# Neighbour layer of a four-layer convolution kernel: one banded matrix per source row, and one shifting transfer per direction

## What is computed

```python
avg = mean(x, axis=channels)
df = abs(conv3x3(avg, laplacian, zero_padding))
k = 1 + round((df - min(df)) / (max(df) - min(df) + 1e-8) * 7)   # per position, min and max per image
patches = unfold3x3_reflect(x)                 # B, C, 9, P
sim = sum_c(x/|x| * patches/|patches|)         # B, 9, P: cosine of each position with its 9 neighbours
w = exp(sim) for the k most similar neighbours, else 0
w = w / sum(w)
enhanced = sum_k(patches * w) + group_norm16(x, gn_weight, gn_bias)
layer1 = enhanced + w2 @ relu(w1 @ enhanced + b1) + b2
```

## Time and profile before

| | |
|---|---|
| median of 3 runs | 5874.34 us (5872.79 to 5879.55) |
| profiled execution, its own time | 5873.65 us |
| its span, first to last instruction | 5871.9 us |
| mean granted TensorE clock | 0.907 of full speed |
| layer 1 in the span | about 2575 to 3600 us |
| TensorE matmuls busy in the whole span | 82% |
| VectorE busy in the whole span | 70% |

### The profile page before, as it was taken

The page is one execution under the profiler, slowest core; times in us unless marked ns, Lnnn a source line. Parts: engine busy times, 40 slices in busy tenths (PEclk is TensorE's granted clock), DMA queues, the critical chain, the costliest instruction groups (busy, mean ns, idle before and its releaser), DMA issues. The chain is left out here.

```text
span 5871.9 us, 127208 instructions
## 1 busy us (share of the span) xinstructions
PE 4826.6 (82%) x46150; PEld 3795.6 (65%) x46150; DVE 4095.5 (70%) x7785; ACT 3137.9 (53%) x5832; POOL 2837.5 (48%) x2148
## 2 busy tenths in 40 slices
PE   2887878787878787842876875999997999999996
PEld 1655555555656565622544543777777999999996
DVE  5767777776767777767987956999984555555554
ACT  1666666565656566641433424666653544456664
POOL 1535454453535454432543524888882333333364
PEclk9888989898988898965988987999998999999998
DMA  4000000000000000022433421011103000000357
GB/s 146 16 31 16 31 16 31 16 25 22 21 26 17 26 20 16 16 70 91 133 124 102 134 70 53 35 46 41 43 32 134 0 0 0 0 0 0 29 49 151
DMA packets 359128, 268.74 MB, mean 46 GB/s; under 512 B 289440, under 2 KB 290720, under 8 KB 352544
## 3 DMA queue, kind: packets, MB, share of 16 engines
q1 hardware_dynamic: 355264, 258.30, 15.4%
q10 hardware_dynamic: 3424, 4.59, 0.2%
HBM read 156.27 MB, written 67.11 MB: 38 GB/s over the span
## 5 line engine op out<-in xcount | busy, mean ns | idle before, releaser
L527 POOL TENSOR_TENSOR l_probs<-l_probs,l_inv 128x1024 f32<-128x1024 f32 x256 | 492.5, 1929 | 570.3 <-DVE l_inv L937 569.8
L1967 POOL TENSOR_TENSOR l_sum<-l_sum,l_prod 128x1024 f32<-128x1024 f32 x224 | 538.6, 2405 | 111.3 <-ACT l_prod L2064 92.8
L2147 DVE SCALAR_TENSOR_TENSOR l_acc<-l_xpad,l_w,l_acc 128x1024 f32<-128x1024 f32 x448 | 574.5, 1289 | 14.8 <-ACT l_acc L2048 1.3
L606 PEld LDWEIGHTS l_upper<-l_rows_T,l_hats 128*64 128x64 f32 x16384 | 516.1, 142 | 86.8 <-issue 85.0
L773 ACT ACTIVATE l_probs<-l_probs,l_shift 128x256 f32<-128x256 f32 x1024 | 506.9, 496 | 103.6 <-DVE l_shift L922 102.0
L606 PE MATMUL l_upper<-l_rows_T,l_hats 128*64 128x64 f32 x16384 | 551.4, 227 | 0.2 <-issue 0.2
L513 POOL TENSOR_TENSOR l_hats<-l_table,l_place 128x256 f32<-128x256 f32 x256 | 180.4, 705 | 765.4 <-PE l_upper L606 393.2
L590 PE MATMUL l_lower<-l_hats,l_rpe 32*128 32x256 f32 x4096 | 316.1, 425 | 262.6 <-issue 119.7
L517 POOL TENSOR_TENSOR l_hats<-l_table,l_place 128x1024 f32<-128x1024 f32 x256 | 498.7, 1948 | 0.0
L898 DVE TENSOR_SCALAR l_hats<-l_hats 128x1280 f32<-128x1280 f32 x256 | 373.2, 1458 | 168.7 <-ACT l_hats L751 168.5
L2559 DVE TENSOR_TENSOR l_sums_ps<-l_conv_odd,l_even_part 128x256 f32<-128x256 f32 x250 | 108.1, 432 | 453.4 <-PE l_conv_odd L2357 405.5
(11 more groups left out here) (325 smaller groups left out, 11891.6 us busy)
## 6 DMA issues: line engine op xcount, KB each, us to landing
l_xleft<-l_xt SPq DMA_DIRECT2D x64, 283.5 KB
l_xright<-l_xt SPq DMA_DIRECT2D x64, 283.5 KB
stat_xs<-in_x SPq DMA_DIRECT2D x8, 2048.0 KB, 23.0
l_hats<-in_x SPq DMA_DIRECT2D x8, 2048.0 KB, 7.7
l_xraw<-in_x SPq DMA_DIRECT2D x8, 2048.0 KB, 8.8
after_layer<-l_xraw SPq DMA_DIRECT2D x64, 256.0 KB, 2.0
l_xblk<-after_layer SPq DMA_DIRECT2D x32, 512.0 KB, 5.0
l_xsum<-after_layer SPq DMA_DIRECT2D x32, 512.0 KB, 5.6
```

What stands on the lines that cost most here:

```text
L527: pool.tensor_tensor(part, part, inv[:, u, cols].rearrange("c (j o) -> c j o", o=1).to_broadcast([C, 4, KEYS]), ALU.mult).then_inc(scaled_ ...
L606: last = pe.matmul(bank[4 + half][64 * s:64 * s + 64, n * UNITS:(n + 1) * UNITS], xhat(ky)[:, k * W:(k + 1) * W], rows_T[:, ky % 2, k, 64 ...
L1967: pool.tensor_tensor(part33(blk), part33(blk), rows(prod33[:, j % PRODUCTS, :]), ALU.add).then_inc(added33, 1)
L2147: last = dve.scalar_tensor_tensor(acc, src, tap, acc, op0=ALU.mult, op1=ALU.add)
```

## The change

The three diagonal matrices of a source row become one banded matrix. `band` is 1 where target column and source column differ by at most 1. Since three neighbouring target columns have three different residues modulo 3, a tile `wres[source column, source row, target row offset, target column modulo 3]` names the weight of each band element; `by_residue` makes it at the start of passes 1 to 4 with nine VectorE operations of 198 elements, in three groups that wait for each other. `build` then writes `[128, n, 66]` elements, and `gather` has two matmuls for a source row where it had six. The shifts of a step become two transfers of 127 partitions, `xleft[1:128] <- src[0:127]` and `xright[0:127] <- src[1:128]`. They do not reflect the edge columns and cross the border between the images; the four affected dots are overwritten later by moves of column transfers. The column transfers at the end of a pass go from 24 to 18 (6 on SP, 12 on ACT). In the setup, GpSimd clears both buffers of `xleft` and `xright` (2304 elements a partition each) and makes `band` and `is_third` in place of `diag`.

```diff
@@ -1062,8 +1062,12 @@
...
         edge = mem.sbuf("edge", [C, 4])
-        diag = mem.sbuf("diag", [C, 3, W])
-        wdiag = mem.sbuf("wdiag", [C, 9 * ROWS * W])
+        THIRDS = -(-W // 3)
+        BAND = 3 * THIRDS
+        band = mem.sbuf("band", [C, BAND])
+        residue = mem.sbuf("residue", [C, 3])
+        wres = mem.sbuf("wres", [C, H + 2, 3, 3])
+        wband = mem.sbuf("wband", [C, 3 * ROWS * BAND])
         gdiag = mem.sbuf("gdiag", [C, 2, C])
...
@@ -1092,6 +1096,7 @@
...
             tmp = smem.sbuf("tmp", [C, B])
+            is_third = smem.sbuf("is_third", [C, 3, THIRDS])
             ps = smem.psum("ps")
...
@@ -1120,9 +1125,12 @@
...
                 pool.memset(edge[:, :], 0.0)
+                pool.memset(xleft[:, :, :, :], 0.0)
+                pool.memset(xright[:, :, :, :], 0.0)
                 pool.memset(inv_avg[:, :, :, :], 0.0)
                 pool.memset(wsrc[:, :, :, :], 0.0)
-                chain.link(pool.memset(diag[:, :, :], 0.0))
+                pool.memset(band[:, :], 1.0)
+                chain.link(pool.memset(is_third[:, :, :], 0.0))
...
@@ -1130,10 +1138,14 @@
...
+                    for sign in (-1, 1):
+                        part = band[64 * b:64 * b + 64, :]
+                        chain.link(pool.affine_select(out=part, in_=part, compare_op=ALU.is_ge, fill=0.0, base=1,
+                                                      pattern=[[sign, BAND]], channel_multiplier=-sign))
                     for k in range(3):
-                        part = diag[64 * b:64 * b + 64, k, :]
-                        chain.link(pool.affine_select(out=part, in_=part, compare_op=ALU.not_equal, fill=1.0, base=-(k - 1),
-                                                      pattern=[[-1, W]], channel_multiplier=1))
+                        part = is_third[64 * b:64 * b + 64, k, :]
+                        chain.link(pool.affine_select(out=part, in_=part, compare_op=ALU.not_equal, fill=1.0, base=-k,
+                                                      pattern=[[-3, THIRDS]], channel_multiplier=1))
                     for col, at in ((0, 0), (2, W - 1)):
...
@@ -1192,6 +1204,7 @@
...
                 dve.tensor_scalar(edge[:, 3:4], edge[:, 2:3], -1.0, 1.0, ALU.mult, ALU.add)
+                dve.reduce_sum(residue[:, :], is_third[:, :, :], axis=LX)
...
@@ -1233,8 +1246,8 @@
...
         stored = [mem.sem(f"stored{u}") for u in range(2)]
-        SHIFTS = 8 * 16
-        NCOLS = 24 * 16
+        SHIFTS = 2 * 16
+        NCOLS = 18 * 16
         WS = 4 * 16
...
@@ -1250,8 +1263,8 @@
...
             widths = [targets(r)[1] + 1 - targets(r)[0] for r in range(SOURCES)]
-            start = sum(widths[:s]) * 3 * W
-            return wdiag[:, start:start + widths[s] * 3 * W].rearrange("p (d j x) -> p d j x", d=3, x=W)
+            start = sum(widths[:s]) * BAND
+            return wband[:, start:start + widths[s] * BAND].rearrange("p (j x) -> p j x", x=BAND)
...
@@ -1298,12 +1311,8 @@
...
                 src = rows_of(t, c * ROWS, ROWS + 1)
-                for b in range(2):
-                    p = 64 * b
-                    sp.dma_start(xleft[p + 1:p + 64, u, :, :], src[p:p + 63]).then_inc(shifted[u], 16)
-                    sp.dma_start(xleft[p:p + 1, u, :, :], src[p + 1:p + 2]).then_inc(shifted[u], 16)
-                    sp.dma_start(xright[p:p + 63, u, :, :], src[p + 1:p + 64]).then_inc(shifted[u], 16)
-                    sp.dma_start(xright[p + 63:p + 64, u, :, :], src[p + 62:p + 63]).then_inc(shifted[u], 16)
+                sp.dma_start(xleft[1:C, u, :, :], src[0:C - 1]).then_inc(shifted[u], 16)
+                sp.dma_start(xright[0:C - 1, u, :, :], src[1:C]).then_inc(shifted[u], 16)
...
@@ -1346,20 +1355,17 @@
...
                     sp.wait_ge(cols_ready, t + 1)
-                    for b in range(2):
-                        p = 64 * b
-                        lo, hi = slice(p, p + 63), slice(p + 1, p + 64)
-                        first, second, but1, last = (slice(p + q, p + q + 1) for q in (0, 1, 62, 63))
-                        moves = [
-                            (inv_avg[hi, 0, 0, 1:H + 1], inv_avg[lo, 0, 1, 1:H + 1]),
-                            (inv_avg[hi, 1, 0, 1:H + 1], inv_avg[lo, 1, 1, 1:H + 1]),
-                            (inv_avg[lo, 0, 2, 1:H + 1], inv_avg[hi, 0, 1, 1:H + 1]),
-                            (inv_avg[lo, 1, 2, 1:H + 1], inv_avg[hi, 1, 1, 1:H + 1]),
-                            (inv_avg[first, 0, 0, 1:H + 1], inv_avg[second, 0, 1, 1:H + 1]),
-                            (inv_avg[last, 0, 2, 1:H + 1], inv_avg[but1, 0, 1, 1:H + 1]),
-                        ]
-                        for to, of in moves:
-                            sp.dma_start(to, of).then_inc(cols_shifted, 16)
+                    at_x = lambda x: slice(x, x + W + 1, W)
+                    moves = [
+                        (inv_avg[at_x(0), 0, 0, 1:H + 1], inv_avg[at_x(1), 0, 1, 1:H + 1]),
+                        (inv_avg[at_x(W - 1), 0, 2, 1:H + 1], inv_avg[at_x(W - 2), 0, 1, 1:H + 1]),
+                    ]
+                    for p in (0, W):
+                        lo, hi = slice(p, p + W - 1), slice(p + 1, p + W)
+                        moves += [(inv_avg[hi, :, 0, 1:H + 1], inv_avg[lo, :, 1, 1:H + 1]),
+                                  (inv_avg[lo, :, 2, 1:H + 1], inv_avg[hi, :, 1, 1:H + 1])]
+                    for to, of in moves:
+                        sp.dma_start(to, of).then_inc(cols_shifted, 16)
...
@@ -1450,12 +1456,10 @@
...
                     first, final = targets(s)
-                    for dx in range(3):
-                        for b in range(2):
-                            at = slice(64 * b, 64 * b + 64)
-                            last = pe.matmul(gather_ps[u][b][:, (s - 2 + first) * W:(s - 1 + final) * W], stage[at, u, s, :],
-                                             matrices(s)[at, dx, :, :].rearrange("p j x -> p (j x)"), start=False,
-                                             stop=(s == SOURCES - 1 and dx == 2))
+                    for b in range(2):
+                        at = slice(64 * b, 64 * b + 64)
+                        last = pe.matmul(gather_ps[u][b][:, (s - 2 + first) * W:(s - 1 + final) * W], stage[at, u, s, :],
+                                         matrices(s)[at, :, 0:W], start=False, stop=(s == SOURCES - 1))
                     last.then_inc(row_done, 1)
...
@@ -1603,20 +1607,22 @@
...
                     act.wait_ge(summed, (t + 1) * STEPS)
-                    for b in range(2):
-                        p = 64 * b
-                        lo, hi = slice(p, p + 63), slice(p + 1, p + 64)
-                        first, second, but1, last = (slice(p + q, p + q + 1) for q in (0, 1, 62, 63))
-                        moves = [
-                            (dots[hi, 3, :], dots[lo, 5, :]),
-                            (dots[first, 3, :], dots[first, 5, :]),
-                            (dots[lo, 8, 0:H - 1], dots[hi, 0, 1:H]),
-                            (dots[last, 8, 0:H - 1], dots[but1, 2, 1:H]),
-                            (dots[hi, 6, 0:H - 1], dots[lo, 2, 1:H]),
-                            (dots[first, 6, 0:H - 1], dots[second, 0, 1:H]),
-                        ]
-                        for to, of in moves:
-                            act.dma_start(to, of).then_inc(cols_shifted, 16)
+                    at_x = lambda x: slice(x, x + W + 1, W)
+                    moves = [
+                        (dots[at_x(0), 3, :], dots[at_x(0), 5, :]),
+                        (dots[at_x(0), 0, :], dots[at_x(0), 2, :]),
+                        (dots[at_x(0), 6, 0:H - 1], dots[at_x(1), 0, 1:H]),
+                        (dots[at_x(W - 1), 5, :], dots[at_x(W - 2), 5, :]),
+                        (dots[at_x(W - 1), 2, :], dots[at_x(W - 1), 0, :]),
+                        (dots[at_x(W - 1), 8, 0:H - 1], dots[at_x(W - 2), 2, 1:H]),
+                    ]
+                    for p in (0, W):
+                        lo, hi = slice(p, p + W - 1), slice(p + 1, p + W)
+                        moves += [(dots[hi, 3, :], dots[lo, 5, :]),
+                                  (dots[lo, 8, 0:H - 1], dots[hi, 0, 1:H]),
+                                  (dots[hi, 6, 0:H - 1], dots[lo, 2, 1:H])]
+                    for to, of in moves:
+                        act.dma_start(to, of).then_inc(cols_shifted, 16)
                     act.wait_ge(sims_ready, t + 1)
...
@@ -1638,10 +1644,23 @@
...
                     wait(dve, row_done, (g - 1) * SOURCES + (s + 1))
-                    dve.tensor_tensor(matrices(s),
-                                      diag[:, :, :].rearrange("p d (o x) -> p d o x", o=1).to_broadcast([C, 3, n, W]),
-                                      wsrc[:, first:final + 1, :, bass.ds(c * ROWS + s, 1)].rearrange("p j d o -> p d j o")
-                                      .to_broadcast([C, 3, n, W]), ALU.mult).then_inc(diag_built, 1)
```

(16 more changed lines are left out.)

## The result

The changed kernel takes **6834.86 us**, median of 4 runs (6831.87 to 6836.04); the kernel before, on the same chip, 5874.9 (5872.79 to 5879.55). The ratio is 1.163 (95% interval 1.161 to 1.165). The forecast was 6840. The profiled execution took 6834.01 us, its span is 6832.3.

The account below looks back on a forecast made before the run. The shifts were taken to decide, both 127-partition transfers on one shared DMA engine (0.85). Terms 256 + 741 - 51 + 15 + 5 = +966 against 5873.65 gave 6840 us, range 6700 to 7130.

Parts of the forecast that it names:

- The other end: Long shifts in passes 0 to 3: one engine at 18.6 GB/s, 31.4 us a transfer, 7483 us in all; chance 0.03.
- 1. pass 0: Pass 0, first shift to end of sums: from 122.8 to 379 us, +256.
- step, pass 0: One step of pass 0: two long transfers, 44.5 us, plus 1.25 us for a wide transfer, 45.8 us.
- 2. passes 1 to 3: Passes 1 to 3: each from 174.3 to 421 us with steps of 49.5 us, +247 each, +741.
- 3. pass 4: Pass 4, no shifts, bound by PE: gather from 9.55 to 3.2 us a step, -51.
- 4 and 6. between passes: Between passes: `by_residue` 3.8 us on the path four times, +15, and fewer column transfers on SP, 0.
- 5. setup, start of layer 1: Setup ahead of layer 1: two memsets on POOL at 2.3 us each, the band's selects about 0.5, +5.
- Part 6: Column transfers at pass ends: SP has 6 instead of 12, but ACT's 12 set the end; 0.
- the lower end: Column transfers at pass ends: the low bound given for their effect, -2 us a pass.
- The faster rival: Shifts: a 127-partition transfer spreads over many engines, DVE sets steps of 14.6 to 15.2 us, 5696 us; chance 0.09.

Follow-up runs that it names:

- E3: The changed kernel with each 127-partition shift cut into 112 and 15 partitions; 5741.35 us, ratio 0.978.
- E7: The changed kernel with each 127-partition shift cut into 126 and 1 partitions; 5752.43 us, ratio 0.979.
- E1: The kernel before with only the new shifts, their column transfers and the two memsets, its matrices and gather kept; 6859.83 us, ratio 1.168.
- E2: The changed kernel with the eight shifts and 24 column transfers of before and without the two memsets; 5795.64 us, ratio 0.986.
- E8: The kernel cut at 112 partitions, with GpSimd doing an eighth of its two products and two sums in layer 1; 5679.32 us, ratio 0.966.
- E6: The kernel cut at 112 partitions, with builds 2 to 4 and 5 to 6 merged into one instruction each; 5720.21 us, ratio 0.973.
- E5: The changed kernel with the `xright` transfer issued from ACT's queue in place of SP's; 6818.17 us, ratio 1.160.

## Why the prediction was right

**The mechanism.** That 63 partitions had gone to nine engines was read from a share of 0.52 to 0.56, and one engine for 127 was worked out from it. The chip shows 0.06. The Trainium skill's rule in "DMA: Bandwidth & Descriptors", section "Why a DMA increments its semaphore by 16 and not by 1", gives the same and is borne out at 127 (0.06) and 122 (0.13). With only shifts in flight in pass 0, the kernels cut at 112 and at 126 show this (E3, then E7):

```profile
2614.00:2616.00 2.00, 0.00 (x0) 0.00 (x0) 2.00 (x2) 0.00 (x0) 0.00 (x0) 0.50 1.00 300
```

```profile
2616.00:2618.00 2.00, 0.00 (x0) 0.00 (x0) 1.75 (x2) 0.14 (x1) 0.00 (x0) 0.50 0.84 272
```

1.00 is sixteen engines, and 0.84 is between thirteen and fourteen of them, where the rule gives fourteen.

**The rate.** 26.3 GB/s for one engine was taken from the input loads; the stretches show 26 and, for two, 53. The other end, 18.6, isn't what one engine has by itself. But it is what each has where many carry shifts: 300 GB/s over sixteen in E3 are 18.8, as 18.6 over nine in the kernel before. Why it falls so was not tried, and the prediction's reason for taking 26.3 (rows read and written beside each other, slow issue) is not shown by any run. That choice was the right one, and it is worth 643 us of the forecast (6840 against 7483).

**Term by term.** Where the parts end is read as before.

| part | forecast | measured |
|---|---|---|
| 1. pass 0 | 379 us, +256 | 379.1 (2588.1 to 2967.2), +256 |
| step, pass 0 | 45.8 | 45.8 (45.95, 45.68) |
| 2. passes 1 to 3 | 421 us, +741 | 419.1, 423.0, 422.4; +735 |
| 3. pass 4 | steps of 12.3 us, -51 | 12.96, -45 |
| 4 and 6. between passes | +15 | +9 |
| 5. setup, start of layer 1 | +5 | +2.4 |
| sum of the terms | +966 | +957 |
| whole span | +966 | +960.4 |

Passes 1 to 3 of before took 174.3, 177.1 and 177.9 us: all three were set equal to the first, which made part 2 by 6 us too large. Of the changed kernel the three passes sum to 1264.5 us, where 1263 were forecast; from one multiplication with `xleft` to the next they were 49.4 to 51.2 us, and the last of each pass 47.2 to 47.8, in place of 49.5.

The total is closer than its terms: the forecast was 6 us too high between the passes, 6 too low in pass 4, 6 too high in passes 1 to 3 and 3 too high in the setup, so errors of some 20 us add up to 9, and in the whole span to 6. That part is luck; the mechanism and the price of a step are not.

**Pass 4** is a mis-sized term: the start of three steps on PE, after.

```profile
4428.11 1.98 PE L1449 MATMUL l_gather_ps<-l_xsum,l_gdiag 128*128 128x512 f32 x4
...
4441.07 1.98 PE L1449 MATMUL l_gather_ps<-l_xsum,l_gdiag 128*128 128x512 f32 x4
...
4454.03 1.98 PE L1449 MATMUL l_gather_ps<-l_xsum,l_gdiag 128*128 128x512 f32 x4
```

12.96 us a step, where 18.6 less 6.4 makes 12.2. The step fell by 5.7 us. In pass 4 the gather's matmuls are busy for 31.5 us, 3.9 a step, where 9.55 before less 6.4 would leave 3.2: a third of the instructions isn't quite a third of the time.

**`by_residue`** and the first work behind it, on DVE's timeline:

```profile
3008.67 0.98 DVE L1660 TENSOR_SCALAR l_wres<-l_wsrc,l_residue 128x198 f32<-128x198 f32 x3 [4.85 <-DMA l_wsrc<-l_rank_or_wout]
3009.69 3.10 DVE L1662 SCALAR_TENSOR_TENSOR l_wres<-l_wsrc,l_residue,l_wres 128x198 f32<-128x198 f32 x6
3012.83 0.48 DVE L1670 TENSOR_SCALAR l_gdiag<-all_ident,l_gscale 128x128 f32<-128x128 f32 x2
```

It takes 4.16 us, against 3.8. The chain between passes grew from about 42.9 to 45.1 us though, only 2.2 a pass, so some 2 us came back. They are the column transfers, and here the prediction read the wait wrongly. DVE's first work behind these transfers, and SP's part of them, before:

```profile
2927.57 8.80 SPq L1362 DMA_DIRECT2D l_inv_avg<-l_inv_avg  x12
...
2937.52 0.15 DVE L1706 COPY l_inv_avg<-l_inv_avg 128x1 f32<-128x1 f32 x1 [9.91 <-DMA l_inv_avg<-l_inv_avg]
```

and after, at the end of pass 1:

```profile
3433.56 4.50 SPq L1368 DMA_DIRECT2D l_inv_avg<-l_inv_avg  x6
...
3441.62 0.15 DVE L1725 COPY l_inv_avg<-l_inv_avg 128x1 f32<-128x1 f32 x1 [8.03 <-DMA l_dots<-l_dots]
```

Part 6 says that ACT's twelve set the end of this wait, and takes 0. Before, SP's twelve did: they start later and land last. Six of them take 4.50 us in place of 8.80, so now ACT's are last (8.3 us at three of the four ends, 8.99 at the first), and DVE waits 1.9 us less. The two edits apart agree: with the transfers alone (E1) the chain is 40.75 us at three of the four ends and 41.54 at the first, with `by_residue` alone (E2) 46.9 to 47.2. The -2 a pass was given as the lower end.

The setup's +2.4 us is counted from the start of the span. Layer 1 itself began 1.95 us earlier than before (GpSimd's first memset at 2564.91 us against 2566.86), for a cause outside the change, and its first shift 2.4 us later, so the setup grew by 4.4 us, near the 5 forecast. A memset of 2304 elements took 2.02 us in place of 2.3.

**What the work saved was worth.** The prediction gave the banded matrices nothing in passes 1 to 3 as long as the shift sets the step, and E1 bears it out: the whole change is only 25 us below it, near the 45 of pass 4 less the 17 that `by_residue` costs in four goes. The faster rival's time is what the prediction reached least well. It put a step without long shifts at 14.6 to 15.2 us, set by DVE, and the kernel at 5696; E3, which is that case, took 5741. Most of its steps are 15.3 us, and in E8, where nearly all are, PE sets them, whose work was put at 14.2. Much of the rest is E3's long steps: the builds were taken by size alone, 3.0 us for ten, where ten take 6.3 beside GpSimd, so that DVE falls behind now and then, PE waits, and PE's clock falls. The loss of the change didn't hang on that term, but the expectations of E2 and E3 did, and they missed.

## To carry to other kernels

Ahead of merging transfers, work out the number of partitions of each and its largest divisor up to 16: a merge from 63 to 127 partitions took the shifts from nine engines to one, and a cut at 112 gave back 1093 us. Read the DMA share in a stretch where nothing else is in flight, in sixteenths, and the rate beside it. When a banded or otherwise smaller operand makes many short VectorE instructions with two inputs, don't price them by size if GpSimd works beside them; fewer and longer ones cost less here (E6). And look at single steps ahead of the mean: E2's passes come to 20 us a step, but its steps are mostly either 15.3 or some 22.4 us.

## What was unexpected of the hardware

**Issuing itself stalls.** On SP's queue in pass 1 of the changed kernel (start, us, queue, line, transfer):

```profile
3114.58 17.05 SPq L1315 DMA_DIRECT2D l_xright<-l_xt  x1
3131.67 22.04 SPq L1334 DMA_DIRECT2D after_layer<-l_res  x1
3153.76 2.73 SPq L1304 DMA_DIRECT2D l_xblk<-after_layer  x1
3156.54 3.22 SPq L1329 DMA_DIRECT2D l_xsum<-after_layer  x1
3159.80 3.45 SPq L1322 DMA_DIRECT2D l_xres<-after_layer  x1
```

The store of 512 KB takes 22.04 us to issue and `xright` 17.05, where issues of shifts in the kernel before took 0.55 to 0.95 us. 22 us is what one long transfer needs on its engine. So behind a transfer on one engine the issuing queue stands too, and with it all that SP has to issue. It isn't only a queue's own transfer that holds it: in E5, with `xright` on ACT's queue, a block load took 42.08 us to issue on SP's (at 2613.09), about two long transfers. By this reading the stall cost little beyond the shift, since the same engine sets the step; the prediction had only the order of the queue. Whether a transfer that doesn't use that engine would be let past wasn't tried.

**VectorE beside GpSimd.** The mean build was 344 ns with most of GpSimd's work left out, and 632 ns beside all of it (E8, E3). In the changed kernel itself it is 505, perhaps since the long waits pull the two engines' work apart; that was not tried.

**The clock behind a wait.** In E3, TensorE waited for 3.20 and 1.93 us; its granted clock was 1.00 in the 5 us with the first of these waits and 0.55 in the next 5, and the step came out 7.5 us longer than the next one.
